# Experts of a sparse feed-forward layer: tokens gathered by quarter rows and transposed by VectorE in 32x32 blocks instead of by TensorE

## The reference

```python
x = x + xattn(layernorm(x), ctx, mask, ...)
h = layernorm(x)                                   # 4096 x 1024
logits = h @ gate_weight.T                         # 64 experts
topk_w, topk_idx = top_k(softmax(logits), 8); topk_w /= topk_w.sum(-1)
g = ragged_dot(sorted_tokens, w_gate, group_sizes) # 1024 -> 384
u = ragged_dot(sorted_tokens, w_up, group_sizes)
out = ragged_dot(silu(g) * u, w_down, group_sizes) # 384 -> 1024
x = x + sum_k topk_w * out
```

## Time and profile before

| | |
|---|---|
| median of 3 runs | 6763.86 us |
| the profiled execution, its own time | 6763.85 us |
| its span, first to last instruction | 6762.0 us |
| TensorE busy in the span | 98% |
| VectorE, ScalarE, GpSimd busy | 49%, 43%, 17% |
| DMA, mean over the span | 155 GB/s |
| experts' first transpose to the last | 2845.6 to 6737.5 us |

### The profile page before, as it was taken

The page is one execution under the profiler, slowest core; times in us unless marked ns, Lnnn a source line. Parts: engine busy times, 40 slices in busy tenths (PEclk is TensorE's granted clock), DMA queues, the critical chain, the costliest instruction groups (busy, mean ns, idle before and its releaser), DMA issues.

```text
span 6762.0 us, 107799 instructions
## 1 busy us (share of the span) xinstructions
PE 6614.3 (98%) x34530; PEld 5884.0 (87%) x34531; DVE 3302.4 (49%) x4252; ACT 2933.3 (43%) x3606; POOL 1147.4 (17%) x1015
## 2 busy tenths in 40 slices
PE   9999998999999999699999999999999999999998
PEld 7888887887888788599989999999999999999998
DVE  4443324999999899732443334322422323323333
ACT  3321224888888644432443334322422333333333
POOL 1000000000000155511211211111111212111121
PEclk9999999999999999899999999999999999999999
DMA  8853555555555666455676566654644556556555
GB/s 257 231 197 143 155 143 145 129 127 128 128 129 128 182 171 171 128 156 130 178 211 172 152 174 189 160 137 106 186 106 106 134 134 162 148 147 162 155 153 152
DMA packets 733960, 1048.19 MB, mean 155 GB/s; under 512 B 301281, under 2 KB 531425, under 8 KB 733858
## 3 DMA queue, kind: packets, MB, share of 16 engines
q0 software_dynamic: 109792, 368.12, 23.5%
q1 hardware_dynamic: 467680, 381.55, 22.1%
q10 hardware_dynamic: 156386, 297.29, 13.0%
HBM read 724.43 MB, written 322.31 MB: 155 GB/s over the span
## 4 chain that ended last, share of the span: by engine, by line
PE 51%; DMA 4%; issue 1%; ACT 1%; DVE 1%; ACTq 0%; SPq 0%; POOLq 0%; DVEq 0%
PE moe_ps_y L1332 5%; PE moe_ps_gate L1345 5%; PE moe_ps_gate L1346 5%; PE moe_ps_gate L1347 5%; PE moe_ps_up L1347 5%; PE moe_ps_up L1346 5%; PE moe_ps_up L1345 5%; PE moe_ps_y L1334 5%; PE moe_ps_y L1333 5%; DMA out<-moe_y,moe_rec_s 2%; PE moe_ps_xT L1322 2%; PE moe_ps_hT L1353 1%; DMA moe_rec_s<-table 1%; DMA first_raw<-in_w_up 1%; ACT moe_gu_hi L1375 0%
## 5 line engine op out<-in xcount | busy, mean ns | idle before, releaser
L1449 DVE SCALAR_TENSOR_TENSOR moe_hidden<-moe_silu,moe_rec_w,moe_ps_up 128x384 f32<-128x384 f32 x286 | 175.8, 615 | 1384.6 <-PE moe_ps_up L1347 1190.3
L1345 PE MATMUL moe_ps_gate<-moe_gu_hi,moe_xT_hi 128*128 128x384 f32 x2288 | 793.4, 347 | 11.1 <-DVE moe_xT_lo L1442 7.5
L1300 POOL DMA_INDIRECT out<-moe_y,moe_rec_s x287 | 478.2, 1666 | 1909.9 <-DMA moe_rec_s<-table 1037.5
L1346 PE MATMUL moe_ps_gate<-moe_gu_lo,moe_xT_hi 128*128 128x384 f32 x2288 | 768.1, 336 | 0.0
L1347 PE MATMUL moe_ps_gate<-moe_gu_hi,moe_xT_lo 128*128 128x384 f32 x2288 | 767.8, 336 | 0.0
L1347 PE MATMUL moe_ps_up<-moe_gu_hi,moe_xT_lo 128*128 128x384 f32 x2288 | 765.1, 334 | 0.0
L1345 PE MATMUL moe_ps_up<-moe_gu_hi,moe_xT_hi 128*128 128x384 f32 x2288 | 764.2, 334 | 0.0
L1346 PE MATMUL moe_ps_up<-moe_gu_lo,moe_xT_hi 128*128 128x384 f32 x2288 | 764.2, 334 | 0.0
L1332 PE MATMUL moe_ps_y<-moe_d_hi,moe_hT_hi 128*128 128x512 f32 x1722 | 696.5, 404 | 3.0 <-DVE moe_hT_lo L1455 3.0
L1334 PE MATMUL moe_ps_y<-moe_d_hi,moe_hT_lo 128*128 128x512 f32 x1722 | 677.2, 393 | 0.0
L1333 PE MATMUL moe_ps_y<-moe_d_lo,moe_hT_hi 128*128 128x512 f32 x1722 | 669.6, 389 | 0.0
(11 more groups left out here) (202 smaller groups left out, 13975.2 us busy)
## 6 DMA issues: line engine op xcount, KB each, us to landing
first_raw<-in_w_gate ACTq DMA_DIRECT2D x63, 1536.0 KB, 9.6
first_raw<-in_w_up ACTq DMA_DIRECT2D x63, 1536.0 KB, 14.7
moe_raw_d<-in_w_down ACTq DMA_DIRECT2D x63, 1536.0 KB, 7.1
proj_a_raw<-in_ctxT POOLq DMA_DIRECT2D x64, 512.0 KB, 5.1
kst<-proj_o SPq DMA_DIRECT2D x256, 128.0 KB, 2.7
vst<-proj_o SPq DMA_DIRECT2D x64, 512.0 KB, 2.6
qst<-proj_o SPq DMA_DIRECT2D x256, 128.0 KB, 2.2
att_kt<-kst SPq DMA_DIRECT2D x64, 512.0 KB, 3.6
```

Source lines behind the costliest of these rows:

```text
L1300: nc.gpsimd.indirect_dma_start(out=acc[:, :], out_offset=bass.IndirectOffsetOnAxis(ap=rec_s[:].bitcast(I32)[:, 0:1], axis=0), in_=y[:], in ...
L1345: nc.tensor.matmul(o[:, 0:I], xT_hi[:, c], gu_hi[:, b, k, c], start=(c == 0), stop=False)
L1346: nc.tensor.matmul(o[:, 0:I], xT_hi[:, c], gu_lo[:, b, k, c], start=False, stop=False)
```

## The change

It touches `output_pass` in two places and `experts_pass` throughout.

In `output_pass` `h2` is written with its features in another order: the 1024 features are 8 chunks of 4 groups of 32 (j, s, a), and they are stored as 4 quarters of 8 x 32 (s, j, a). The router's matrix is loaded in the same order, in 8 loads instead of one, so the logits are the same.

In `experts_pass` a tile's 128 tokens are 4 groups of 32. `tokens` is now filled by four gathers, each of 128 quarter rows (1 KB): partition block k gets quarter k of the tokens of group g in the columns of g. For this the records are loaded four times, once per partition block, with the 4 groups side by side (`record_groups`), and GpSimd works out the row numbers (4 x token + quarter) before the gathers. VectorE then transposes `tokens` in one instruction, in 32x32 blocks, into `turned` in PSUM (`turn_tokens`), two tiles ahead. `tokens_high` and `tokens_low` read it through a pattern of four dimensions in runs of 32. TensorE's 8 transposes per tile go; `tokens_high` now waits for the end of the tile's up product (it overwrites `xT_hi`), where before it waited for the transposes behind it. The transposes of `hidden` stay.

```diff
-                for dst, src in ((gamma_sb, row_broadcast(gamma, H)), (beta_sb, row_broadcast(beta, H)),
-                                 (gate_sb, gateT.rearrange("(c p) e -> p c e", p=P))):
+                for dst, src in ((gamma_sb, row_broadcast(gamma, H)), (beta_sb, row_broadcast(beta, H))):
                     pool.dma_start(dst[:], src).then_inc(consts_in, 16)
+                gate_rows = gateT.rearrange("(c s a) e -> c a s e", s=G, a=W)
+                for c in range(C):
+                    rows = slice(c % G * W, (c % G + 1) * W)
+                    pool.dma_start(gate_sb[rows].rearrange("a (s h) e -> a h s e", s=G)[:, c // G], gate_rows[c]).then_inc(consts_in, 16)
...
-                        nc.scalar.activation(h2[:, 1 - b], x1[:, 1 - b], ACT.Identity, bias=shift[:],
+                        nc.scalar.activation(by_quarter(h2[:, 1 - b]), in_chunks(x1[:, 1 - b]), ACT.Identity, bias=shift[:],
...
+        turned, y_ps = s.ps("turned", [P, H]), s.ps("y", [P, H])
+        xT_ps = turned[:].rearrange("p (g j b) -> p j g b", g=G, b=W)
...
+                def record_groups(rows):
+                    for k in range(G):
+                        sp.dma_start(rec_g[k * W:(k + 1) * W], rows.rearrange("(g b) w -> b g w", b=W)).then_inc(rec_g_in, 16)
...
                 def tile(t, is_first=False):
+                    sp.wait_ge(hidden_done, t + 2)
+                    sp.sem_inc(sp_passed, 1)
+                    record(rec_w, t + 1, rec_w_in)
                     if not is_first:
                         sp.wait_ge(added, 16 * t)
                     sp.sem_inc(sp_passed, 1)
                     record(rec_s, t - 1, rec_s_in)
-                    sp.wait_ge(hidden_done, t + 2)
+                    sp.wait_ge(rows_done, t + 4)
                     sp.sem_inc(sp_passed, 1)
-                    record(rec_w, t + 1, rec_w_in)
-                    sp.wait_ge(gathered, 16 * (t + 3))
-                    sp.sem_inc(sp_passed, 1)
-                    record(rec_g, t + 3, rec_g_in)
+                    record_groups(record_rows(t + 4))
...
                 def gather(t):
-                    pool.wait_ge(rec_g_in, 16 * (t + 1))
-                    pool.wait_ge(xT_done, t)
+                    pool.wait_ge(rec_g_in, 16 * G * (t + 1))
+                    pool.wait_ge(turned_done, t)
                     pool.sem_inc(pool_passed, 1)
-                    nc.gpsimd.indirect_dma_start(
-                        out=f32(tokens[:]), out_offset=None, in_=h2st[:, :],
-                        in_offset=bass.IndirectOffsetOnAxis(ap=rec_g[:].bitcast(I32)[:, 0:1], axis=0)).then_inc(gathered, 16)
+                    nc.gpsimd.tensor_scalar(rows[:], rec_g[:].bitcast(I32)[:, :, 0], float(G), group[:], ALU.mult, ALU.add).then_inc(rows_done, 1)
+                    pool.wait_ge(rows_done, t + 1)
+                    pool.sem_inc(pool_passed, 1)
+                    for g in range(G):
+                        nc.gpsimd.indirect_dma_start(
+                            out=tokens[:, g * (H // G):(g + 1) * (H // G)], out_offset=None, in_=h2_quarters,
+                            in_offset=bass.IndirectOffsetOnAxis(ap=rows[:, g:g + 1], axis=0)).then_inc(gathered, 16)
...
+                gather(2)
                 with pool.Fori(0, last_tile + 1) as t:
-                    gather(t + 2)
+                    gather(t + 3)
                     add(t - 1)
...
-                    transpose_tokens(t + 1)
                     down(t - 1, b_before)
...
                 def tokens_high(t):
-                    act.wait_ge(xT_done, t + 1)
-                    nc.scalar.copy(xT_hi[:], xT_ps).then_inc(xT_hi_done, 1)
+                    act.wait_ge(turned_done, t + 1)
+                    if not (isinstance(t, int) and t == 0):
+                        act.wait_ge(gu_done, 2 * t)
+                    nc.scalar.copy(by_group(xT_hi), xT_ps).then_inc(xT_hi_done, 1)
...
+                def turn_tokens(t):
+                    dve.wait_ge(gathered, 16 * G * (t + 1))
+                    if not (isinstance(t, int) and t == 0):
+                        dve.wait_ge(xT_lo_done, t)
+                    nc.vector.transpose(turned[:], tokens[:]).then_inc(turned_done, 1)
...
                     tokens_low(t + 1)
+                    turn_tokens(t + 2)
                     if e is not None:
                         split(e, b, 0, GU)
```

More of the change, by code:

```diff
@@ L61, in f32, with in_chunks, by_quarter @@
     return ap.bitcast(F32)
+def in_chunks(rows):
+    return rows.rearrange("p (j s a) -> p j s a", s=G, a=W)
+def by_quarter(rows):
+    return rows.rearrange("p (s j a) -> p j s a", s=G, a=W)
 def row_broadcast(dram_row, n):
@@ L1182, in experts_pass @@
         d_hi, d_lo = s.sb("d_hi", [P, 2, CI, H], F32R), s.sb("d_lo", [P, 2, CI, H], F32R)
-        tokens, xT_hi, xT_lo = s.sb("tokens", [P, H], F32R), s.sb("xT_hi", [P, C, P], F32R), s.sb("xT_lo", [P, C, P], F32R)
+        tokens, xT_hi, xT_lo = s.sb("tokens", [P, H]), s.sb("xT_hi", [P, C, P], F32R), s.sb("xT_lo", [P, C, P], F32R)
         silu, hidden = s.sb("silu", [P, I]), s.sb("hidden", [P, I])
@@ L1243, in _, with record_rows @@
                 last_tile = sp.value_load(dir_sb[0:1, last_at:last_at + 1], min_val=E - 1, max_val=MAX_TILES - 2)
+                def record_rows(t):
+                    row = sp.value_load(dir_sb[0:1, bass.ds(row_at + 1 + t, 1)], min_val=0, max_val=table.shape[0] - P)
+                    return table[bass.ds(row, P), :]
                 def record(dst, t, sem):
-                    row = sp.value_load(dir_sb[0:1, bass.ds(row_at + 1 + t, 1)], min_val=0, max_val=table.shape[0] - P)
-                    sp.dma_start(dst[:], table[bass.ds(row, P), :]).then_inc(sem, 16)
-                for t in range(2):
-                    sp.wait_ge(gathered, 16 * (t + 1))
-                    record(rec_g, t + 1, rec_g_in)
+                    sp.dma_start(dst[:], record_rows(t)).then_inc(sem, 16)
+                for t in range(3):
+                    sp.wait_ge(rows_done, t + 1)
+                    record_groups(record_rows(t + 1))
                 def tile(t, is_first=False):
+                    sp.wait_ge(hidden_done, t + 2)
+                    sp.sem_inc(sp_passed, 1)
+                    record(rec_w, t + 1, rec_w_in)
                     if not is_first:
@@ L1316, in _ @@
                 pe.sem_inc(hT_done, 1)
-                pe.wait_ge(ready, 2)
-                def transpose_tokens(t):
-                    pe.wait_ge(gathered, 16 * (t + 1))
-                    for c in range(C):
-                        last = nc.tensor.transpose(xT_r[:, c], tokens[:, c * P:(c + 1) * P], ident_r[:])
-                    last.then_inc(xT_done, 1)
+                pe.wait_ge(ready, G + 1)
                 def down(t, b):
@@ L1458, in _ @@
                 dve.sem_inc(hT_lo_done, 1)
+                for k in range(G):
+                    nc.vector.memset(group[k * W:(k + 1) * W], float(k)).then_inc(ready, 1)
                 nc.vector.memset(f32(d_hi[:, 1]), 0.0).then_inc(zeroed, 1)
```

37 lines of the change are left out of this document (22 added, 15 removed).

## The result

The changed kernel took **6711.43 us** (median of 4 runs, 6710.70 to 6714.65), the kernel before 6764.45 on the same chip: a ratio of 0.9921, 95% interval 0.9906 to 0.9937. It is faster by 53 us, not by the forecast 176, and lies 6 us outside the range. The profiled execution took 6714.65 us with a span of 6713.0, where the kernel before had 6762.0: 49 less.

A forecast was written before the change was run, and what follows sets the result against it. The prediction took TensorE, busy 98%, to bound the kernel. Terms -200 (transposes) + 15 (first tiles) + 4 (start) + 3.4 (end) + 2 (router) = -176 us gave 6588 us, range 6563 to 6705.

The forecast's parts named there:

- the sum for an expert's first tile: VectorE's split tile: 3.6 us in hand, less 0.7 + 0.7 and 1.2, leaves about 1.0; +15 us put on 63 tiles.
- rival A: Gather loop: slow gathers or landings make VectorE wait, delaying `hT_lo` in experts' first tiles; 6680 us, chance 0.14.
- theory 2: Explanation proposed after measuring, not forecast: VectorE waits for the four gathers to land, and everything behind its transpose is late.
- Transposes: TensorE, each tile: removing eight token transposes saves 0.70 us, 286 times, -200 us (-183 to -203).
- VectorE's transpose: VectorE, each tile: takes 1.2 us, hidden under w_down and the next gate product, costing nothing in an ordinary tile.
- Gathers: GpSimd, each tile: four gathers 1.28 us apart; the loop closes with 2.1 to 3.3 us in hand, costing nothing.
- Add: GpSimd, each tile: the add starts up to 3.5 us later, costing nothing in the steady tile.
- Start and router: Before the first expert tile, +4 us (2 to 7); router's eight loads in place of one, +2 us (0 to 7).
- End: Kernel's end: the last adds go behind a useless gather, +3.4 us (0 to 6).
- C: Rival: runs of 32 double `xT_hi` and `xT_lo`, so TensorE waits 0.4 us a tile; 6708 us, chance 0.05.
- B: Rival: the gather loop fails to close in ordinary tiles, slower than before; 7420 us, or about 7090; chance 0.10.
- D: Rival: TensorE does not give back 0.64 us a tile, waiting for `hT_lo` or `y` before w_down; 6773 us, chance 0.03.

The follow-up runs named there:

- no weight loads: Changed kernel, with the weight loads of experts after the first only signalled as done and old weights reused, splits kept: 6587.31 us.
- one gather by `rows`: Changed kernel with one gather of whole 4 KB rows, indexed by a column of `rows`, in place of four quarter gathers; other tokens computed: 6603.51 us.
- rows ahead: Changed kernel, with GpSimd computing row numbers once the last gather has landed, during VectorE's transpose; only the gathers wait for the transpose: 6690.30 us.
- before, add late: Kernel before the change, with twelve idle GpSimd memsets between gather and add: 6936.93 us.
- The two edits on ScalarE's queue: Changed kernel with the load of w_down moved behind the next expert's first silu and `hT_hi` rounded ahead of the copy of `y`: 6653.39 us.
- The run with the add between gathers: Changed kernel, with GpSimd issuing the previous tile's add between the second and third of the four gathers: 7058.75 us.

## Why the prediction was wrong

The add that goes out beside an expert's split (the expectations call it the add in a first tile), in the kernels that leave ScalarE's order as it is and whose gathers and records were not held up by the edit itself; medians, from the start of the tile that TensorE is in, the landing counted to the last event on the add's semaphore:

| kernel | starts at, us | lands after, us | back at, us | time, us |
|---|---|---|---|---|
| before | 4.4 | 9.8 | 14.5 | 6764 |
| changed | 10.2 | 8.9 | 19.1 | 6711 |
| no weight loads | 8.8 | 6.3 | 15.1 | 6587 |
| one gather by `rows` | 5.1 | 6.3 | 11.5 | 6604 |
| rows ahead | 8.8 | 9.1 | 17.8 | 6690 |
| before, add late | 9.8 | 9.3 | 19.0 | 6937 |

The copy of `y` could begin at 12.8 us (the next tile's start, as in the ordinary tile). Back at some 15 us the landing costs little, at 19 it stalls TensorE for 4 us behind short experts. **The step that failed** is the sum for an expert's first tile. Of the add the prediction says "its landing is wanted by the copy of `y` a tile later, and w_down wants that copy 8 us on. Cost in the steady tile: nothing", and in the steady tile that holds. The sum for the first tile then counts VectorE's room alone and does not come back to the add. There the copy that waits for it holds up on ScalarE `hT_hi`, w_down's split, the next load and the next silu: the prediction asked who reads the copy, and not what stands behind it. Nor does that sum ask how long an add takes to land: beside a weight load it is 9 to 10 us. The term "I put 15 us on the 63 such tiles (0.24 each), between 0 and 63 x 1.1 = 69" measured 140.1: 113.5 of it behind the 27 experts of one to three tiles, 4.2 each, 13.3 behind those of four, and 9.5 in the very first expert, by rival A's wait. An estimated 51 of it is the lower clock that follows a stall, for which the prediction had no term. The two edits on ScalarE's queue alone bring 58 back without touching GpSimd or VectorE; theory 2 has no place for that. It is right in one thing: late tokens delay the next gathers and the next add. How much of the 140 runs over that loop was not parted.

Point by point:
- *Transposes*: -200 forecast, -195.5 measured; the tile 12.80 and 12.81. Right.
- *VectorE's transpose*: 1.2 taken from the row of the same size, 1.26 measured. The figures of the Trainium skill, "VectorE: DVE Perf Modes", section "The three transpose paths", had given an estimate of 2.49; the trace has half of that. The advice of that page's rules to take TensorE for a 128x128 transpose did not fit this case: 0.69 us of the engine that sets the time were bought for 1.26 us of one that is busy 55%.
- *Gathers*: 1.25 to 1.34 apart for 1.28. The loop's "2.1 to 3.3 us in hand" was too much: the first gather starts 0.84 behind the end of the row numbers, which I had not counted, and VectorE waited for tokens 113 times. The run with the add between gathers shows how little is left.
- *Add*: "up to 3.5 us later" was 4.0 in an ordinary tile and 5.8 beside a split, where the row numbers took 1.54 beside the split. The Trainium skill, "SBUF — State Buffer", section "Who interferes with whom", says that a VectorE instruction with two SBUF inputs contends with a GpSimd instruction that reads SBUF. The trace agrees, with row numbers of 1.54 for 0.27 and a gather of 1.74 for 0.95 beside the split in the stall shown. Beside VectorE's transpose, which has one input, the row numbers took 0.27 (the run with the row numbers ahead).
- *Start and router*: +6 forecast, +3.2 measured. *End*: +3.4 and +3.3.
- *Rivals*: A named the place (first tiles) and gave 6680, but by VectorE waiting for tokens and TensorE for `hT_lo`, in 63 tiles alike, and TensorE waited for `hT_lo` in five places; C's 6708 is near the result by accident: `xT_hi` takes 1.01 and `xT_lo` 1.23 as before. B's loop closes in the changed kernel, and fails to when 1.9 us are added to it. D falls with the tile of 12.81.
